# The first chunk of a Mamba scan and the end of a graph attention layer, reordered in a four-layer graph network kernel

## Chip, cores and metric

One Trainium2 chip, one of its cores. The metric is the device time of one execution in microseconds (us); a kernel is told by the median of its runs.

## The reference, cut to what matters

Four layers, each followed by a residual and a layer norm. N is 2048 nodes, the width is 128, all float32. The change touches the end of layer 2 (a dense graph attention) and layer 3 (a graph convolution that feeds a Mamba block).

```
def _L2_gnn_ref(h, adj, weight, a_l, a_r, b):
    x = h @ weight
    scores = (x @ a_l)[:, None] + (x @ a_r)[None, :]
    attn = jnp.where(adj != 0, jnp.exp(leaky_relu(scores, 0.2)), 0.0)
    return attn / jnp.maximum(attn.sum(-1, keepdims=True), 1e-12) @ x + b

def _L3_gnn_ref(x, adj, ...):            # D_INNER 256, D_STATE 16, DT_RANK 8, D_CONV 4
    h = layernorm(relu(adj @ x @ gcn_w + gcn_b)) * ln_g + ln_b
    xc, z = split(h @ w_in)
    u = silu(causal_conv(xc, conv_w) + conv_b)
    dbc = u @ w_xp                       # 8 columns for dt, 16 for B, 16 for C
    dt = softplus(dbc[:, :8] @ w_dt + b_dt)
    hst = exp(dt * A) * hst + dt * B * u # over the 2048 rows, 256 channels x 16 states
    y = sum over states(hst * C) + u * D_skip
    return (y * silu(z)) @ w_out

x = layernorm(x + _L2_gnn_ref(...)); x = layernorm(x + _L3_gnn_ref(...))
```

## The kernel before, in words

The order of the work is written out by hand for each engine: TensorE (PE), VectorE (DVE), ScalarE (ACT), GpSimd (POOL) and the DMA queue of SyncE (SP). Each engine runs its own list in order, and semaphores (`then_inc`, `wait_ge`) tie the lists together.

**Layer 2.** For each of 16 tiles of source nodes `jt`, ACT and DVE make a tile `q2[jt % 4]` of attention weights (128 x 2048), and PE multiplies it into the sums of all 16 output tiles `it` (L899, 128 x 129: the 129th column is the row's sum of weights). The sums lie in PSUM banks 0 to 5, three output tiles to a bank. `l2_mm` is counted up for each bank in the pass of the last `jt`. Then `norm(2, ...)` on DVE works by quarters of four tiles: `after_layer2(q)` forms the factors `zi` and adds the scaled sums to `X` (L1236 to L1243), the statistics follow (L1132, L1135), ACT makes the root (L480, L482), and the scaled rows are `x_ready` (ACT, L486, for quarters 0 to 2; DVE, L1120, for quarter 3). The quarter's rows are scaled only behind the next quarter's residual. Quarter 0 waits for two banks, quarter 1 for all six.

**Layer 3.** The rows are cut into four chunks of 512. `a_part(c, ...)` on PE is adj @ x for a chunk (L913: 16 products of 128 x 512), `a_copy`, `gcn`, `relu`, `h_spread` (statistics, DVE L1263, L1266), `inverse_root` (ACT L589, L591), a scaling (`h_rescale` on DVE for chunk 0, `h_scale` on ACT, L624, for the later ones, with offsets from the DVE's `offset`, L1289), `h_fill` (transposes), `ht_copy` (L596), `conv_part` (L939: 4 taps for each of two blocks of 128 channels), `u_out` (L605), `dbc_product`, `dbc_copy`, `dt_product` (L965), and softplus as `dt_abs` (L665), `dt_log` (L671, L673) and `softplus` (DVE, L1301).

The recurrence runs in steps `k`: 16 states in each of 4 chunks, 64 in all (`n` is the step within its chunk). It needs dt and dt*u "doubled": each block of 64 channels stands in both halves of the 128 partitions, since one instruction handles two states. `dt2` and `du2` are those copies. Before the change both are made by DMA (`by_blocks`): four transfers for each block of 128 channels of dt, on ACT's queue in chunk 0 and SP's later, and as many for du = dt*u on SP's queue. A step is: `decay` on ACT (L688, twice), `make_dbu` on POOL (L445), `scan` on DVE (L1318, twice), `weigh` by C (DVE L1329, or POOL L457 for 3 steps in 8), and `add_up` on PE (L1006). For DVE's `weigh` PE spreads the row of C over the partitions (`spread`, L987), from three bfloat16 `piece`s of dbc that are taken off one after another (`take_off`, L959).

PE, ACT and DVE carry the preparation of the next chunk (`next_chunk`) and of the chunk after it (`chunk_after`, `a_part` in the portions `cuts`) between the steps; what goes at which step `n` is a hand-written table. At the start of a chunk `gated` (L1358) reads the finished sums, then `y_done` lets PE start the next chunk's sums with the skip products (L997), and `out_product` (L976), `residual` and an `o_scale` finish the old chunk.

Of the kernel before, what the change touches and what calls it, by code (L numbers as in the profile page):

```python
# [14 lines left out]
P = 128  # L15
N = 2048
NT = N // P
# [34 lines left out]
def gnn_program(nc, t, out):  # L52
    ctx = ExitStack()
    with ctx:  # L54
# [147 lines left out]
        dt2_in, du2_in = [sem("dt2_in%d" % b) for b in range(DI)], [sem("du2_in%d" % b) for b in range(DI)]  # L202
# [58 lines left out]
        w_dt = wt[:, 11:13, :].rearrange("p a m -> p (a m)")  # L261
# [48 lines left out]
        def doubled(done, c, b):  # L310

            return done[b] if c == 0 else done[0], 64 * (c + 1)
        HF_BANKS = (4, 5, 7)

        def act_features(jt):

            return sum(i % 4 < 2 for i in range(jt + 1))

# [3 lines left out]
        def later_loads(sp):  # L322
# [16 lines left out]
            sp.dma_start(w_dt[96:96 + DTR, :], t["L3_gnn_w_dt"]).then_inc(w4_in, 16)  # L339
            sp.dma_start(w_dt[96 + DTR:97 + DTR, :], t["L3_gnn_b_dt"].rearrange("(o f) -> o f", o=1)).then_inc(w4_in, 16)  # L340
# [32 lines left out]
            for c in range(NCH):  # L373
                sp.wait_ge(dbc_ev, c + 1)
                sp.dma_start(b_dram[c], dbc[0:2 * STATES, :]).then_inc(b_out, 16)
                sp.wait_ge(b_out, 16 * (c + 1))
                if c == 0:
                    b_rows(c, 0)
                    for b in range(DI):
                        sp.wait_ge(du_ready, b + 1)  # L380
                        by_blocks(sp, du, du2[0], slice(b, b + 1), du2_in[b])
                    sp.wait_ge(a_mm, 2)
                else:
                    sp.wait_ge(dt_ready, 2 * c + 2)
                    if c >= 2:
                        sp.wait_ge(da_ready, 2 * STATES * (c - 1))
                    by_blocks(sp, dt_, dt2[c % 2], slice(0, DI), dt2_in[0])
                    sp.wait_ge(du_ready, 2 * c + 2)
# [13 lines left out]
        def later_pool(pool):  # L402
# [22 lines left out]
            def make_du(c, b):  # L425

                pool.wait_ge(dt_ready, 2 * c + b + 1)
                pool.wait_ge(u_ready, 2 * c + b + 1)
                if c:
                    pool.wait_ge(*doubled(du2_in, c - 1, b))  # L430
                nc.gpsimd.tensor_tensor(du[:, b, :], dt_[:, b, :], u[:, b, :], ALU.mult).then_inc(du_ready, 1)

            def make_dbu(k):
# [3 lines left out]
                if n < 2:  # L437
                    pool.wait_ge(*doubled(du2_in, c, n))
# [21 lines left out]
            for b in range(DI):  # L460
                make_du(0, b)
            for k in range(3):
                make_dbu(k)
            for k in range(STEPS):
# [7 lines left out]
        def later_act(act):  # L472
# [126 lines left out]
            def u_out(c, b, bank):  # L599

                act.wait_ge(conv_mm, 2 * c + b + 1)
                if c:
                    act.wait_ge(du_ready, 2 * c)
                    act.wait_ge(skip_mm, c)
                nc.scalar.activation(u[:, b, :], PS[:, bank, :], ACT.Silu, bias=conv_b[:, b:b + 1]).then_inc(u_ready, 1)  # L605
# [14 lines left out]

            def shift_and_scale(dst, v, first, count, offsets, done):
# [6 lines left out]
            def h_scale(c, bank):  # L628

                act.wait_ge(h_off, c)  # L630
                shift_and_scale(ag_tiles, PS[:, bank, :].rearrange("p (s f) -> p s f", f=P), 4 * c, 4, dj, h_ready)

            def o_scale(c):

                act.wait_ge(o_off, c + 1)
                shift_and_scale(xo[c], xo[c], 4 * c, 4, bj, x_ready)

            def dbc_copy(c, bank):
# [3 lines left out]
                if c:  # L642
                    act.wait_ge(b_out, 16 * c)
                    act.wait_ge(dt_mm, 2 * c)
# [14 lines left out]
            def dt_abs(c, b, bank):  # L659

                act.wait_ge(dt_mm, 2 * c + b + 1)
                if c:
                    act.wait_ge(du_ready, 2 * c)
                    act.wait_ge(*doubled(dt2_in, c - 1, b))
                nc.scalar.activation(dt_[:, b, :], PS[:, bank, :], ACT.Abs).then_inc(sp_abs, 1)  # L665

            def dt_log(c, b):

                act.wait_ge(sp_abs, 2 * c + b + 1)
                v = dt_[:, b, :]  # L670
                nc.scalar.activation(v, v, ACT.Exp, scale=-1.0).then_inc(sp_exp, 1)  # L671
                act.wait_ge(sp_exp, 2 * c + b + 1)
# [6 lines left out]
            def decay(j):  # L679
# [4 lines left out]
                if n < 2:  # L684
                    act.wait_ge(*doubled(dt2_in, c, n))
# [19 lines left out]
            for b in range(DI):  # L705
                dt_abs(0, b, 6 + b)
            for b in range(DI):
                dt_log(0, b)
                act.wait_ge(dt_ready, b + 1)
# [1292 lines left out]
```

## Time and profile before

| | |
|---|---|
| median of 3 runs | 933.14 us (932.04 to 934.73) |
| time of the profiled execution | 937.67 us |
| its span | 935.8 us |
| busy: PE, DVE, ACT, POOL | 824.3, 690.8, 508.2, 231.0 us |

The span is what the instructions cover; 1.87 us of the profiled execution lie around it. Layer 2's products run from 555.6 us to 616.9 us of the span, layer 3 from 622.1 us to its end. An engine's time between two of its instructions is idle, and the square brackets in a row say how long it was and whose work ended it.

### The profile page before, as it was taken

How to read it: one execution, taken by the hardware profiler on the slowest of the kernel's cores; microseconds unless marked ns; L12 is line 12 of the kernel's file. 1: busy time of each engine (PE TensorE's matmuls, PEld its weight loads, DVE VectorE, ACT ScalarE, POOL GpSimd, SP SyncE). 2: the span in 40 equal slices, each digit the busy share in tenths (PEclk: the TensorE clock that was granted, in tenths of full speed). 3: DMA queues.
4: the chain of work that ended last, by engine and by line, in shares of the span. 5: the costliest groups of instructions: out<-in, count | busy, mean ns of one | idle time of the engine just before them, and what ended most of it. 6: DMA issues, size and time to landing. Idle time of an engine off the chain costs nothing. (4 is left out here: it accounts for less than half of the span.)

```text
span 935.8 us, 11963 instructions
## 1 busy us (share of the span) xinstructions
PE 824.3 (88%) x4196; PEld 523.5 (56%) x4196; DVE 690.8 (74%) x975; ACT 508.2 (54%) x802; POOL 231.0 (25%) x132
## 2 busy tenths in 40 slices
PE   6999988999999999999599989979579889787755
PEld 6755537888888888854354569954223333231211
DVE  2986889999999999427843148851177888989897
ACT  2654537777877777535220147522457666666461
POOL 2000000000000000000020010001368887877992
PEclk9999998999999999999699979989779999897777
DMA  8589975221122021069100000000432715517210
GB/s 278 189 314 330 360 283 224 91 91 44 46 90 90 0 90 45 1 278 423 47 1 0 1 0 1 1 23 1 115 90 58 159 34 139 123 35 164 64 45 11
DMA packets 39360, 102.42 MB, mean 109 GB/s; under 512 B 6122, under 2 KB 11132, under 8 KB 32788
## 3 DMA queue, kind: packets, MB, share of 16 engines
q1 hardware_dynamic: 38116, 100.55, 32.6%
q10 hardware_dynamic: 1200, 1.32, 0.5%
q8 instruction: 23, 0.38, 0.2%
q14 instruction: 21, 0.17, 0.1%
HBM read 75.33 MB, written 18.14 MB: 100 GB/s over the span
## 5 line engine op out<-in xcount | busy, mean ns | idle before, releaser
L1752 PE MATMUL PS<-big 128*128 128x256 f32 x768 | 194.4, 385 | 3.9 <-ACT big L1582 3.8
L221 PE MATMUL PS<-ident,big 128*128 128x128 f32 x1123 | 158.5, 281 | 22.4 <-DMA big<-in_L_gnn_weight 7.3
L221 PEld LDWEIGHTS PS<-ident,big 128*128 128x128 f32 x1123 | 136.9, 146 | 47.2 <-issue 21.3
L445 POOL TENSOR_TENSOR big<-big 128x1024 f32<-128x1024 f32 x64 | 149.9, 2352 | 20.4 <-DVE big L1318 9.2
L1752 PEld LDWEIGHTS PS<-big 128*128 128x128 f32 x768 | 133.9, 191 | 22.1 <-ACT big L1582 7.6
L1582 ACT ACTIVATE big<-PS 128x512 f32<-128x512 f32 x192 | 105.0, 598 | 58.3 <-PE PS L221 57.3
L1318 DVE TENSOR_TENSOR_SCAN big<-PS,stripes,big 128x512 f32<-128x512 f32 x96 | 116.3, 1260 | 3.6 <-POOL big L445 3.1
L404 POOL MEMSET big<- 128x16 f32 x1 | 0.1, 127 | 465.2 <-DVE big L1120 465.2
L1951 DVE SCALAR_TENSOR_TENSOR big<-big,rz 128x2048 f32<-128x2048 f32 x48 | 112.7, 2350 | 0.9
L1929 DVE CUSTOM_DVE_ANT_0 big<-big 128x2048 f32<-128x2048 bf16 x48 | 109.7, 2289 | 0.1
L688 ACT ACTIVATE PS<-big,stripes 128x512 f32<-128x512 f32 x128 | 86.2, 686 | 40.9 <-DVE big L1318 40.4
L1572 ACT ACTIVATE big<-big,ymin 128x2048 f32<-128x2048 f32 x48 | 96.3, 2006 | 15.2 <-DVE ymin L1929 14.9
L1006 PE MATMUL PS<-big,stripes 128*64 128x512 f32 x256 | 79.0, 727 | 19.3 <-DVE big L1329 19.2
L320 ACT ACTIVATE big<-PS 128x512 f32<-128x512 f32 (+3 forms) x51 | 29.9, 592 | 78.4 <-PE PS L780 24.0
L913 PE MATMUL PS<-big 128*128 128x512 f32 x128 | 64.0, 641 | 5.2 <-ACT big L486 5.2
L1329 DVE TENSOR_TENSOR big<-PS,big 128x1024 f32<-128x1024 f32 x41 | 49.5, 1206 | 15.9 <-issue 11.0
L780 PE MATMUL PS<-big 128*128 128x512 f32 x128 | 59.6, 618 | 1.4 <-ACT big L320 1.4
L899 PE MATMUL PS<-big 128*128 128x129 f32 x512 | 59.7, 281 | 1.1 <-DVE big L1224 1.1
L899 PEld LDWEIGHTS PS<-big 128*128 128x128 f32 x512 | 59.3, 197 | 1.4 <-issue 1.4
L1675 PE MATMUL PS<-big 128*128 128x512 f32 x128 | 57.8, 597 | 0.0
L1006 PEld LDWEIGHTS PS<-big,stripes 128*64 128x64 f32 x256 | 16.3, 155 | 67.0 <-issue 34.4
L457 POOL TENSOR_TENSOR big<-big 128x1024 f32<-128x1024 f32 x18 | 42.4, 2355 | 15.4 <-DVE big L1318 15.3
(207 smaller groups left out, 1002.0 us busy)
## 6 DMA issues: line engine op xcount, KB each, us to landing
big<-in_adj SPq DMA_DIRECT2D x16, 2048.0 KB, 9.0
big<-at_dram SPq DMA_DIRECT2D x4, 4096.0 KB, 27.3
at_dram<-big SPq DMA_DIRECT2D x3, 4096.0 KB, 16.6
big<-b_dram SPq DMA_DIRECT2D x32, 256.0 KB, 4.4
big<-big SPq DMA_DIRECT2D x24, 256.0 KB, 4.7
big<-b_dram SPq DMA_DIRECT2D x36, 128.0 KB, 4.0
at_dram<-big SPq DMA_DIRECT2D x1, 3072.0 KB, 18.8
big<-e_dram SPq DMA_DIRECT2D x3, 1024.0 KB, 6.8
```

What stands on the lines that cost most here:

```text
L221: return nc.tensor.transpose(PS[:, bank, col:col + P], src, ident[:])
L445: nc.gpsimd.tensor_tensor(dbu[k % 3], du2[c % 2][:, 2 * (n % 2):2 * (n % 2) + 2, :], bb[group % 2][:, pair_of(k) % 2, :].unsqueeze(1).to_b ...
L688: nc.scalar.activation(PS[:, 5 + j % 3, :], dt2[c % 2][:, q, :], ACT.Exp, scale=na[:, q, pair_of(k):pair_of(k) + 1]).then_inc(da_ready, 1)
L899: m = nc.tensor.matmul(sums(it, slice(0, P + 1)), q2[jt % 4][:, it * P:(it + 1) * P], x2[:, jt, :], start=(jt == 0 and it % 3 == 0), stop= ...
L913: m = nc.tensor.matmul(PS[:, bank, :], X[:, jt, :], AT[:, jt, c * CH:(c + 1) * CH], start=(jt == 0), stop=(jt == NT - 1))
L1006: m = nc.tensor.matmul(PS[h * HALF:(h + 1) * HALF, 2 + n % 2, :], fold, v[:, h, :], start=False, stop=(n >= STATES - 2), skip_group_check= ...
L1318: nc.vector.tensor_tensor_scan(hs[k % 3][:, b, :], PS[:, 5 + j % 3, :], dbu[k % 3][:, b, :], state[:, pair_of(k), 2 * (n % 2) + b:2 * (n % ...
L1572: e = nc.scalar.activation(w[s], w[s], ACT.Exp, bias=ymin[:, s:s + 1], scale=-1.0, accum_out=zsum[:, s:s + 1])
L1582: nc.scalar.activation(qt[v % 4], PS[:, v % 4, :], ACT.Copy).then_inc(qt_ready, 1)
L1752: m = nc.tensor.matmul(PS[:, 4 + k // 3, 0:256], hw[:, jt, h, :], qt[v % 4][:, 256 * c:256 * c + 256], start=(h == 0 and jt == 0), stop=(h ...
L1929: m = nc.vector.tensor_tensor_reduce(out=w[s], in0=bm[2 * pair + j], in1=eb[0][h], scale=1.0, scalar=3.0e38, op0=ALU.add, op1=ALU.min, acc ...
L1951: m = nc.vector.scalar_tensor_tensor(w[s], w[s], rz[:, s:s + 1], aw[pair][:, j, :], ALU.mult, ALU.mult)
```

## The change

It touches four places. (1) Layer 2: PE runs the source tiles 0 to 12 as before, then waits for the weights of the last three together and runs them by output tile, so that the banks finish one after another; DVE's quarter `q` waits for the banks that it reads only. (2) First chunk: the weights of dt are loaded with each block of 64 columns twice, and PE computes dt doubled in four products; softplus works on the four, straight in `dt2[0]`. u is doubled by DMA (SP's queue) as soon as it is there, and POOL multiplies it by dt in place (`first_du`). The DMAs of dt on ACT's queue and of du on SP's are gone in chunk 0. (3) DVE's `h_spread(1, 1)` stands behind `weigh(0)` and no longer ahead of the loop. (4) `offset` is computed on ACT (five small instructions) and no longer on DVE; `h_fill`, `conv_part`, `out_product`, `residual` and the portions of `a_part` move by one step `n`, and from chunk 1 on `h_fill` and `out_product` stand ahead of work that they stood behind.

```diff
             for c in range(NCH):
+                if c == 0:
+                    for b in range(DI):
+                        sp.wait_ge(u_ready, b + 1)
+                        by_blocks(sp, u, du2[0], slice(b, b + 1), du2_in[b])
                 sp.wait_ge(dbc_ev, c + 1)
...
                 if c == 0:
                     b_rows(c, 0)
-                    for b in range(DI):
-                        sp.wait_ge(du_ready, b + 1)
-                        by_blocks(sp, du, du2[0], slice(b, b + 1), du2_in[b])
                     sp.wait_ge(a_mm, 2)
...
+            def first_du(q):
+
+                pool.wait_ge(du2_in[q // 2], 64)
+                pool.wait_ge(dt_ready, dt_count(0, q))
+                nc.gpsimd.tensor_tensor(du2[0][:, q, :], dt2[0][:, q, :], du2[0][:, q, :], ALU.mult).then_inc(du_first, 1)
...
-            for b in range(DI):
-                make_du(0, b)
-            for k in range(3):
+            for k in range(2):
+                for b in range(DI):
+                    first_du(2 * k + b)
                 make_dbu(k)
+            make_dbu(2)
...
+            def offset(offsets, root, count, first, done, nth):
+
+                cols = slice(first, first + 4)
+                nc.scalar.activation(offsets[:, cols], mv[:, cols, 0], ACT.Copy, scale=-1.0).then_inc(done, 1)
+                act.wait_ge(root, count)
+                act.wait_ge(done, 2 * nth - 1)
+                for i in range(first, first + 4):
+                    m = nc.scalar.activation(offsets[:, i:i + 1], offsets[:, i:i + 1], ACT.Copy, scale=rstd[:, i:i + 1])
+                m.then_inc(done, 1)
...
-            for b in range(DI):
-                dt_abs(0, b, 6 + b)
-            for b in range(DI):
-                dt_log(0, b)
-                act.wait_ge(dt_ready, b + 1)
-                by_blocks(act, dt_, dt2[0], slice(b, b + 1), dt2_in[b])
-            for p in range(3):
-                piece(0, p, 4)
-            for j in range(3):
-                decay(j)
+            for q in range(3):
+                dt_abs(0, q, FIRST_DT[q])
+                dt_log(0, q)
+                piece(0, q, 4)
+                if q:
+                    decay(q - 1)
+            dt_abs(0, 3, FIRST_DT[3])
+            dt_log(0, 3)
+            decay(2)
             a_copy(1, 1)
             relu(1, 1)
...
-                if n == 0:
+                if n == (1 if c == 1 else 0):
                     inverse_root(h_var, c + 1, 4 * c, 4, h_log, h_root)
-                elif n == 1:
+                    offset(dj, h_root, c + 1, 4 * c, h_off, c)
+                if n == 1:
                     h_scale(c, 1)
...
+            LAST = 3
+            for jt in range(NT - LAST):
                 pe.wait_ge(q2_ready, jt + 1)
                 pe.wait_ge(l2_xev, jt // 4 + 1)
                 for it in range(NT):
...
+            pe.wait_ge(q2_ready, NT)
+            for it in range(NT):
+                for jt in range(NT - LAST, NT):
+                    m = weighted(jt, it)
+                if it % 3 == 2 or it == NT - 1:
+                    m.then_inc(l2_mm, 1)
...
-            for b in range(DI):
-                dt_product(0, b, 6 + b)
+            for q in range(4):
+                dt_product(0, q, FIRST_DT[q])
             pe.wait_ge(sel_ready, 6)
+            a_part(1, 1, 8, 10)
             take_off(0, 0, 4)
-            a_part(1, 1, 8, 9)
+            a_part(1, 1, 10, 12)
             take_off(0, 1, 4)
-            a_part(1, 1, 9, NT)
+            a_part(1, 1, 12, NT)
...
                 if n == 1:
-                    h_fill(c, 1)
-                elif n == 2:
                     if c >= 2:
                         pe.wait_ge(zg_ready, 3 * (c - 1))
-                    conv_part(c, 0, 0, range(0, 1))
+                    h_fill(c, 0)
+                elif n == 2:
+                    conv_part(c, 0, 0, range(0, 2))
                 elif n == 3:
-                    conv_part(c, 0, 0, range(1, 4))
-                elif n == 4:
+                    conv_part(c, 0, 0, range(2, 4))
                     if c >= 2:
                         pe.wait_ge(o_added, c - 1)
-                    conv_part(c, 1, 1, range(TAPS))
+                    conv_part(c, 1, 1, range(0, 1))
+                elif n == 4:
+                    conv_part(c, 1, 1, range(1, TAPS))
...
-            cuts = {6: (0, 2), 7: (2, 4), 8: (4, 6), 9: (6, 9), 10: (9, 12), 11: (12, 14), 12: (14, 16)}
+            cuts = {6: (0, 2), 7: (2, 4), 8: (4, 6), 9: (6, 8), 10: (8, 10), 11: (10, 13), 12: (13, 16)}
...
                 if spreads(k):
                     spread(k)
+                if n == 1 and 0 < c < NCH - 1:
+                    next_chunk(c + 1, n)
                 for i in sums_at(k):
                     add_up(i)
-                if c and n == 2:
+                if c < NCH - 1 and (n != 1 or c == 0):
+                    next_chunk(c + 1, n)
+                if c and n == 1:
                     pe.wait_ge(yg_ready, c)
...
-                if q < 2:
-                    dve.wait_ge(l2_mm, 2 if q == 0 else 6)
+                banks = ((0, 1), (2,), (3,), (4, 5))[q]
+                dve.wait_ge(l2_mm, banks[-1] + 1)
...
-            for b in range(DI):
-                softplus(0, b, 6 + b)
+            for q in range(4):
+                softplus(0, q, FIRST_DT[q])
             scan(0)
-            h_spread(1, 1)
             for k in range(STEPS):
                 c, n = k // STATES, k % STATES
                 if k + 1 < STEPS:
                     scan(k + 1)
                 if not on_pool(k):
                     weigh(k)
+                if k == 0:
+                    h_spread(1, 1)
...
-                if c and n == 3:
+                if c and n == 2:
                     dve.wait_ge(o_mm, c)
...
-                if c and n == 5:
-                    offset(bj, o_root, c, 4 * (c - 1), o_off)
-                if c < NCH - 1:
-                    if n == 0:
-                        offset(dj, h_root, c + 2, 4 * (c + 1), h_off)
-                    elif n == 8 or n == 9:
-                        softplus(c + 1, n - 8, 0)
+                if c < NCH - 1 and (n == 8 or n == 9):
+                    softplus(c + 1, n - 8, 0)
```

## Rows read from the trace of the kernel before

**Rows 1.** The page, part 2: DVE's busy tenths in 40 slices.

```profile
DVE  2986889999999999427843148851177888989897
```

**Rows 2.** Windows: busy time of each engine, then PEclk, DMA share, GB/s.

```profile
656.00:675.00 19.00, 8.65 (x16) 3.08 (x15) 1.49 (x3) 7.52 (x13) 5.91 (x4) 0.66 0.55 141
...
690.00:739.00 49.00, 46.60 (x124) 15.36 (x120) 40.98 (x38) 31.05 (x59) 42.08 (x20) 0.90 0.42 98
...
880.00:925.00 45.00, 29.12 (x86) 7.81 (x87) 44.03 (x45) 22.48 (x35) 36.28 (x16) 0.73 0.13 32
```

**Rows 3.** Timeline, layer 2 and its end: start, duration, what, [idle before, releaser].

```profile
545.73 0.94 PE L221 MATMUL PS<-ident,big 128*128 128x128 f32 x4 [2.61 <-DVE big L1120]
...
589.83 27.08 PE L899 MATMUL PS<-big 128*128 128x129 f32 x241
...
606.88 2.29 DVE L1224 SCALAR_TENSOR_TENSOR big<-big 128x2048 f32<-128x2048 f32 x1 [1.27 <-ACT big L569]
614.78 0.23 DVE L1236 TENSOR_TENSOR zi<-PS,ci 128x3 f32<-128x3 f32 x2 [5.60 <-PE PS L899]
...
620.42 1.65 ACT L486 ACTIVATE big<-big,bj,rstd 128x128 f32<-128x128 f32 x4 [1.73 <-DVE bj L1114]
...
622.12 17.71 PE L913 MATMUL PS<-big 128*128 128x512 f32 x34 [5.21 <-ACT big L486]
...
622.82 1.65 ACT L486 ACTIVATE big<-big,bj,rstd 128x128 f32<-128x128 f32 x4 [0.33 <-DVE bj L1114]
...
639.00 0.60 ACT L320 ACTIVATE big<-PS 128x512 f32<-128x512 f32 x1 [11.71 <-PE PS L913]
```

**Rows 4.** Windows of one microsecond at low PEclk or a change of it (third last number).

```profile
546.00:547.00 1.00, 0.67 (x4) 0.26 (x2) 0.00 (x0) 0.30 (x1) 0.00 (x0) 0.50 0.03 9
...
621.00:622.00 1.00, 0.00 (x0) 0.00 (x0) 0.96 (x8) 1.00 (x4) 0.00 (x0) 0.53 0.00 0
...
627.00:628.00 1.00, 1.00 (x2) 0.34 (x1) 0.67 (x3) 0.26 (x2) 0.00 (x0) 0.56 0.00 0
```

**Rows 5.** Timeline of all engines, the first chunk's dt and first steps.

```profile
659.49 0.60 ACT L665 ACTIVATE big<-PS 128x512 f32<-128x512 f32 x1 [1.31 <-PE PS L965]
...
662.88 2.47 ACTq L307 DMA_DIRECT2D big<-big  x4
...
665.39 0.63 ACT L671 ACTIVATE big<-big 128x512 f32<-128x512 f32 x1 [3.27 <-issue]
...
669.63 2.34 POOL L445 TENSOR_TENSOR big<-big 128x1024 f32<-128x1024 f32 x1 [0.88 <-DMA big<-big]
...
670.66 0.63 PE L959 MATMUL PS<-big,neg 96*96 96x512 bf16 x1 [10.35 <-ACT big L320]
...
674.90 2.34 DVE L1318 TENSOR_TENSOR_SCAN big<-PS,big 128x512 f32<-128x512 f32 x2 [7.49 <-ACT PS L688]
...
684.39 0.89 DVE L1263 BATCH_NORM_STATS2 stats<-PS 128x6 f32<-128x128 f32 x4 [7.15 <-ACT PS L583]
...
690.40 1.50 ACT L624 ACTIVATE big<-PS,dj,rstd 128x128 f32<-128x128 f32 x4 [1.63 <-DVE dj L1289]
...
694.18 2.07 PE L939 MATMUL PS<-es,ns 128*128 128x512 f32 x2 [0.68 <-ACT es L596]
```

**Rows 6.** Timeline by engine: a DVE stall, and the start of chunk 1.

```profile
707.50 1.23 DVE L1329 TENSOR_TENSOR big<-PS,big 128x1024 f32<-128x1024 f32 x1 [3.71 <-issue]
...
750.48 3.54 PE L997 MATMUL PS<-ns,wt 128*128 128x512 f32 x4 [3.69 <-DVEq L1360]
...
750.88 1.50 ACT L624 ACTIVATE big<-PS,dj,rstd 128x128 f32<-128x128 f32 x4 [1.59 <-DVE dj L1289]
...
756.02 1.23 DVE L1329 TENSOR_TENSOR big<-PS,big 128x1024 f32<-128x1024 f32 x1 [0.45 <-DVE big L1318]
...
769.14 1.23 DVE L1329 TENSOR_TENSOR big<-PS,big 128x1024 f32<-128x1024 f32 x1 [1.80 <-issue]
```

**Rows 7.** Groups of instructions by line, 612 us to the end.

```profile
L1289 DVE SCALAR_TENSOR_TENSOR bj<-mv,rstd 128x4 f32<-128x4 f32 x3 | 5.4, 1806 | 0.0
```

## The prediction on record

> **What bounds the kernel now.** I read the page first. DVE is the busiest engine of the last third, and ahead of it, in the three slices from 608 to 679 us, its row falls to 5, 1 and 1 tenths [rows 1]. The chain that ended last covers only the kernel's last steps, so I went by stages and timelines instead. The windows show three regimes: from 656 to 675 no engine is full (PE is busy 8.65 of 19 us, DVE 1.49, ACT 7.52), from 690 to 739 PE is (46.60 of 49), and the last chunk is DVE's (44.03 of 45) [rows 2]. So a microsecond taken from the serial stretches in front counts in full; one given to chunk 0's steps counts only if PE's list is earlier too. All times below are places in the span of before; "earlier" is against them.
>
> **Layer 2's end.** A float32 product stands as two rows, so 241 rows in 27.08 us are 0.225 us a product and 3.6 us a pass of 16 [rows 3]. The products end at 616.9, so the last three passes (48 products, 10.8 us) began at 606.1. The last weights are DVE's at 606.88 + 2.29 = 609.2. New: PE waits for them, 3.1 us idle with nothing to fill it, and ends at 620.0, 3.1 later. But banks 0 and 1 are full after 18 products: 609.2 + 4.05 = 613.25, against 614.78 now [rows 3].
>
> DVE's first quarter then goes as before: 5.64 us from its start to ACT's scaling, which takes 1.65 (614.78 and 620.42 [rows 3]). Inside it the factors of ten columns shrink to three, four instructions still, so I take 0.16 off. `x_ready` comes at 613.25 + 5.5 + 1.65 = 620.4, just after PE's end. PE starts on it at 620.5, not 622.12: 1.6 earlier. The later quarters came 2.4 us apart (620.42 and 622.82 [rows 3]); two new sets of factors (0.9 each, the 614.78 step up to the sums) make it 3.3. At full clock PE eats four products in 3.5, so it does not wait for them.
>
> The clock: the granted clock falls to half (1.2 GHz) at about 621.1 in PE's 5.2 us of idleness, and is back at 2.4 GHz at about 627.9 [rows 4]. PE worked at half rate from 622.1 to 627.9 and lost 2.9 us: 16.9 us up to `a_copy` at 639.00 where 14.0 (0.87 a product) would do. New: this idleness shrinks to 0.5 us, so that loss goes. The 3.1 us of idleness at 606.1 may bring one of its own. In before the clock was at half behind an idleness of 2.61 us, at 546 [rows 3, 4], and behind the 3.69 us ahead of L997, whose four rows took 3.54 us, twice the 0.44 a row of full rate [rows 6]. Both had lighter work in front than full passes. I take that it falls (nearer to the 2.61 and 3.69 than to nothing; 6 in 10), with half rate for some 3.5 us as in that L997 row: 1.7 us lost. Sum: 1.6 + 2.9 - 1.7 = 2.8 earlier. Bounds: 4.5 if it does not fall; 1.5 if it stays low as long as at 622.
>
> The Trainium skill (TensorE: Matmul & The Clock Gate, "Why this matters for your kernels") warns against idle gaps between bursts of matmuls, which bring the clock down. By that rule the new gap is a fault of this change; the rows at 546 and 750 agree as far as they go, though neither is a gap in full passes.
>
> **First chunk: dt and its doubling.** Up to `dbc_copy` nothing changes. ACT's row is now: two `abs`, `exp`, `ln`, then 2.47 us in which it only issues four DMAs, `exp` again at 665.39, DMAs again; PE idles 10.35 us for the first `piece`, DVE scans at 674.90 [rows 5]. New, for one block of dt: `abs` 0.63, `exp` 0.66, `ln` 0.53 to the next, 1.82 in all (0.60 and 0.63 busy [rows 5], plus a semaphore's 0.03). ACT's list from 659.49: four of these, 7.3; three pieces at 0.5 and two decays at 0.6, 2.7; half a microsecond of waiting for `take_off`, behind two products of `a_part`; softplus on DVE 0.7, and 0.2 for its start. That is 670.9: `scan(0)` 4.0 earlier. The two extra dt products cost PE 0.9 each and ACT never waits for them. u's DMAs: its last block is ready about 4 us before 659.49 (dbc products 1.9, copy 0.6, dt product 0.9 and their gaps), the first 3.4 us sooner, a convolution's length: 655.5 and 652.1. Four issues take 2.47, and what was issued up to 665.35 let POOL begin at 669.63 [rows 5], so at most 4.3 to landing: 658.9 and 662.3. POOL needs them at 662.2 and 668.0. They are hidden; the second would cost what it exceeds 668 by. B's rows follow u's on the queue and may come 1 to 2 us later than now, near 666, still before dt*u of state pair 0.
>
> POOL then: dt*u of the last block behind the last softplus, 1.26 (half of the elements of L445 at 2.34 [rows 5], and a little), `make_dbu(1)` 2.34: 674.5. That is a new wait of 1.3 us in front of `scan(1)`, queued on DVE; behind it are `weigh(0)` and `h_spread(1, 1)`. PE: with its 10.35 us filled, `a_part` of chunk 1 ends near 669.4, not 680.9. ACT reaches `a_copy` at 670.7, `relu` ends at 674.1. DVE: `scan(1)` 674.5 to 676.85, `weigh(0)` 1.1, `h_spread` 1.25: 679.2. So DVE's 7.15 us in front of L1263 [rows 5] are gone. ACT: root 0.6, `offset` five small instructions 0.7 (my bound: 0.5 if they pipeline, 1.5 at 0.3 each as dependent ones), `h_scale` 1.5: 682.05, against 690.40 + 1.50 = 691.9. Transposes and `ht_copy` as now: convolution at 684.35 against 694.18 [rows 5]. **9.8 earlier.** Bounds: 8.5 (offset 1.5) and 10.5, the shift of DVE's own list.
>
> **Chunk 0's steps** are PE's. DVE stood 3.71 us for `spread(5)` [rows 6], behind the eight taps. The taps start 9.8 earlier, their number before `spread(5)` is the same, and PE still idles twice for 2.4 us ahead of them, so the clock will be low there again. So 9.8 is kept, no more; `cuts` only moves two products from one gap to another. If the clock stays up, up to 2.6 more.
>
> **Starts of chunks 1 to 3.** `h_fill` now stands ahead of `add_up(16)`. In before `y_done` let PE go at 750.48; `h_scale` ended at 752.4. With `offset` 0.7 in ACT's list instead of DVE's, `h_scale` no longer waits 1.59 [rows 6] and ends at 751.5. So PE starts at 751.5, 1.1 later, then: transposes 1.1 and skip 3.5 at half clock, sums 1.1, `out_product` 2.0: `spread(18)` at 759.5, not 755.9, and DVE's `weigh(18)` waits 4 us instead of 0.45 [rows 6]. Most is not lost: in before DVE waited later, 1.80 us at 769.14 for `spread(21)` [rows 6], behind the same PE work. PE itself is 1.1 later plus the clock's 1.0, less 0.7 of its own waiting for `ht_copy`: about 1.4 later. DVE drops `offset` of 1.8 us (mean 1806 ns [rows 7]) and `dj`'s 0.3 to 1.4, but PE binds chunk 1: -1.0. In chunk 2 PE has no `a_part`, DVE binds: I estimate waits 1.0 longer in all by the same count, against the saved 1.8: +0.8. Chunk 3: `out_product` ahead of `spread(50)` costs DVE 2.0, `offset` returns 1.8: -0.2. Sum -0.4, bounds -3.5 and +2.
>
> **Sum.** 2.8 + 9.8 - 0.4 = 12.2 us. The profiled execution took 937.67 us (span 935.8 and 1.87 around it), so 925.5 for its like; the median of the runs shown is 4.53 lower, 933.14, and gives **920.9 us**.
>
> **Rivals.** (a) The forecast, clock down in layer 2's gap: 920.9, chance 0.5. (b) The clock stays up there: 1.7 more, 919.2; if it also stays up in chunk 0, 916.6. PE was at full work before the gap, which speaks for it: 0.25. (c) The chunk starts give back: PE, 4 us late at each of the two, is not absorbed because the `spread` queue runs full, 3 us a start plus chunk 3's: 920.9 + 5.5 = 926.4. For it: PE 46.60 of 49 us busy; against: the 1.8 us already waited for `spread(21)`. 0.17. (d) The doubling does nothing: POOL is bound by B's rows, which stand behind u's eight DMAs, and `make_dbu(0)` starts where it does, 669.63 [rows 5]. Then the two blocks of dt*u (2.5) and `make_dbu(1)` end at 676.9, 2.4 later than forecast, and DVE with them: 923.3. 0.04. (e) Slower: `h_fill` ahead of `add_up` holds all of PE until `h_scale`, and DVE behind it. It decides from 7.7 us of unabsorbed delay at each of two starts (12.6 + 2.8, halved), where the rows give 1.1 for PE and 4 for DVE; `h_scale` would have to end near 758, so two ACT tasks ahead of it would have to wait for scans that themselves wait. Then 936. 0.04.
>
> The range takes (b)'s lower end, less a microsecond for the bounds of `offset` and the starts, and (c) just: 915.5 to 926.5; outside lie (e), the worse half of (c) and sums of bounds, 0.2. Within 0.3% (2.8 us, what a measurement of this kernel tells from no change) lies little of any case: faster 0.93, same 0.03, slower 0.04.
>
> **What would show it.** PE idle for some 3 us near 606, then L899 by tiles with DVE's L1236 four times; L913 starting within 1 us of L899's end, at 2.4 GHz. No DMA issues on ACT between `ln` and `ln`; first L1318 4 us closer to the first L665 (11.4 us, now 15.4), first L939 of chunk 1 24.9 us after it, now 34.7. `weigh(18)` waiting about 4 us on PE, `weigh(21)` hardly. Wrong it would be if the first L1318 waited for a DMA, if L913 still began at half clock, or if DVE's idle time in chunks 1 and 2 grew by more than the some 7 us of L1289 that it drops.

## The result and the profile after

Six runs of the changed kernel (after, for short) have a median of 925.0 us (921.7 to 929.1); six of the kernel before on the same chip have 933.2 (931.5 to 938.2). The ratio is 0.9908, 95% interval 0.9882 to 0.9934: 8.6 us faster (the medians differ by 8.2), where 12.2 were forecast. The ratios of this document go by means and its medians are medians, so a difference can be read in two ways; where the two disagree both are given. 925.0 lies inside the forecast range, 1.5 us below its upper end. One execution of e5 below took 1245.7 us at a mean granted clock of 0.64 and is left out of every figure.

The profiled execution of after took 921.7 us, its span 919.9, the fastest of the six, and 15.9 less than the span of before. Of that, 5.9 us lie ahead of the changed code: the last attention weights of layer 2 end at 603.27 and not at 609.17 (606.88 + 2.29, [rows 3]), though nothing was changed before them. So places in the span can't be compared between two executions; stretches can. From the end of the last weights to the end of the span it is 326.63 us before and 316.63 after. These **10.0 us** are what this pair of executions gives the change.

The page, part 2, DVE's busy tenths in 40 slices of after (before: [rows 1]):

```profile
DVE  3986989999999999517752338872278878889897
```

The hole is shallower: its three slices read 7, 2 and 2 where they read 5, 1 and 1. The timeline of layer 2's end and the first chunk, for all engines (start, duration, what, [idle before, releaser]):

```profile
603.32 10.98 PE L933 MATMUL PS<-big 128*128 128x129 f32 x96 [3.05 <-DVE big L1272]
607.72 0.23 DVE L1284 TENSOR_TENSOR zi<-PS,ci 128x3 f32<-128x3 f32 x2 [4.45 <-PE PS L933]
613.11 1.65 ACT L505 ACTIVATE big<-big,bj,rstd 128x128 f32<-128x128 f32 x4 [1.48 <-DVE bj L1162]
614.81 10.57 PE L956 MATMUL PS<-big 128*128 128x512 f32 x24 [0.50 <-ACT big L505]
628.85 0.60 ACT L326 ACTIVATE big<-PS 128x512 f32<-128x512 f32 x1 [7.18 <-PE PS L956]
...
648.18 3.69 PE L1009 MATMUL PS<-big,wt 9*128 9x512 f32 x8
649.33 0.60 ACT L697 ACTIVATE big<-PS 128x512 f32<-128x512 f32 x1 [1.31 <-PE PS L1009]
651.80 2.78 PE L956 MATMUL PS<-big 128*128 128x512 f32 x4
655.05 0.59 ACT L326 ACTIVATE big<-PS 96x512 bf16<-96x512 f32 x1 [1.51 <-PE PS L1002]
661.59 2.33 DVE L1359 TENSOR_TENSOR_SCAN big<-PS,big 128x512 f32<-128x512 f32 x2
665.54 2.34 DVE L1359 TENSOR_TENSOR_SCAN big<-PS,big 128x512 f32<-128x512 f32 x2 [1.62 <-POOL big L463]
...
670.96 0.85 ACT L650 ACTIVATE dj<-dj,rstd 128x1 f32<-128x1 f32 x4
675.39 3.78 PE L982 MATMUL PS<-es,ns 128*128 128x512 f32 x4 [0.44 <-ACT es L615]
```

Read it against [rows 3] and [rows 5]. PE waits 3.05 us for the last weights, the new gap, and runs the last three source tiles by output tile. DVE starts at 607.72, 4.4 us behind that. PE's wait ahead of the adjacency products is 0.50 us where it was 5.21. The first scan comes 12.26 us behind the first `abs` (15.41 before), and the first convolution of chunk 1 comes 26.06 behind it (34.69 before). ACT issues no DMA between the logarithms.

The start of chunk 1, timeline of PE and DVE of after:

```profile
730.43 1.21 DVE L1400 TENSOR_TENSOR big<-PS,big 128x1024 f32<-128x1024 f32 x1
733.13 1.09 PE L221 MATMUL PS<-ident,big 128*128 128x128 f32 x4 [5.06 <-ACT big L656]
734.01 3.62 PE L1043 MATMUL PS<-ns,wt 128*128 128x512 f32 x4
738.86 2.05 PE L1020 MATMUL PS<-wt,big 128*128 128x128 f32 x16
740.75 0.38 PE L1031 MATMUL PS<-big,sel 96*128 96x512 bf16 x1
741.22 1.23 DVE L1370 TENSOR_TENSOR big<-PS,big 128x1024 f32<-128x1024 f32 x1 [4.42 <-issue]
```

`h_fill` (L221) waits 5.06 us for `h_scale`. Behind it stand the skip products, the sums and `out_product` (L1020), and only then `spread(18)` (L1031), 10.3 us behind `gated` (L1400). In before it was 6.4 us:

```profile
749.15 1.22 DVE L1358 TENSOR_TENSOR big<-PS,big 128x1024 f32<-128x1024 f32 x1
...
755.54 0.38 PE L987 MATMUL PS<-big,sel 96*128 96x512 bf16 x1
```

DVE's `weigh(18)` waits 4.42 us for it (before 0.45, [rows 6]).

The stretches in one table, each from one landmark to the next, in the profiled execution of each kernel. The first scan lies inside the fourth stretch.

| stretch | before | after | earlier | forecast |
|---|---|---|---|---|
| last weights to first adjacency product | 12.95 | 11.54 | 1.41 | 1.6 less 1.7 for the clock |
| to `a_copy` | 16.88 | 14.04 | 2.84 | 2.9 |
| to first `abs` of dt | 20.49 | 20.48 | 0.0 | 0 |
| to the first convolution of chunk 1 | 34.69 | 26.06 | 8.63 | 9.8 |
| to `gated` of chunk 1 | 54.97 | 55.04 | -0.07 | 0 |
| chunk 1 (`gated` to `gated`) | 63.08 | 66.15 | -3.07 | -1.0 |
| chunk 2 | 63.48 | 63.36 | 0.12 | 0.8 |
| chunk 3 and the end | 60.09 | 59.96 | 0.13 | -0.2 |

### The profile page after: what moved, and what is told of

It is laid out like the page before. It is cut to its first block and busy times, and to the rows that moved or that the text cites. A ratio compares the mean times of both kernels' runs of the same rounds, so it can differ in the third digit from the quotient of the medians.

```text
span 919.9 us, 12005 instructions
## 1 busy us (share of the span) xinstructions
PE 816.0 (89%) x4200; PEld 518.7 (56%) x4200; DVE 686.1 (75%) x977; ACT 515.6 (56%) x838; POOL 233.0 (25%) x134
## 5 line engine op out<-in xcount | busy, mean ns | idle before, releaser
L221 PE MATMUL PS<-ident,big 128*128 128x128 f32 x1123 | 158.8, 282 | 34.4 <-ACT big L656 13.3
L221 PEld LDWEIGHTS PS<-ident,big 128*128 128x128 f32 x1123 | 137.3, 146 | 58.0 <-issue 30.2
L956 PE MATMUL PS<-big 128*128 128x512 f32 x128 | 61.6, 619 | 0.5 <-ACT big L505 0.5
L815 PE MATMUL PS<-big 128*128 128x512 f32 x128 | 58.9, 611 | 1.4 <-ACT big L326 1.4
L1712 PE MATMUL PS<-big 128*128 128x512 f32 x128 | 57.8, 596 | 0.0
```

The source lines that it names most:

```text
L221: return nc.tensor.transpose(PS[:, bank, col:col + P], src, ident[:])
L956: m = nc.tensor.matmul(PS[:, bank, :], X[:, jt, :], AT[:, jt, c * CH:(c + 1) * CH], start=(jt == 0), stop=(jt == NT - 1))
```

## The experiments

In the cuts of code, `...` marks lines left out. Two theories of the shortfall. **Theory A**: the order at the chunk starts costs more than forecast (rival (c) in part), since PE stands for `h_scale` with everything behind it. **Theory B**: the first chunk gives less, since PE's clock falls in it. The rival to both is that layer 2's part gives nothing. The kernel before measured 932.1 us (11 runs) beside e1 to e4, 933.0 (22) beside e5 to e8 and 933.9 (11) beside e9 to e11.

**e1, no change to layer 2.** The changed kernel, with layer 2's end as before.

```
-            for jt in range(NT - LAST):
+            for jt in range(NT):
...
-                dve.wait_ge(l2_mm, banks[-1] + 1)
+                if q < 2:
+                    dve.wait_ge(l2_mm, 2 if q == 0 else 6)
```

> The changed kernel with layer 2's end as before. My theory: layer 2's part is worth 4.3 us in the one profile (1.4 us of an earlier start of the first adjacency product, 2.9 us of clock that is no longer lost), so from the last attention weights to the chunk's first a_copy should be 29.8 us again and not 25.6, with the granted clock at half when the adjacency product begins, and the time about 929. Rival: the clock's part differs from run to run, and only the 1.4 us are steady: 926.5, with a stretch of 27 us.

926.4 us (925.4 to 929.7), ratio 0.9942 (0.9923 to 0.9961). Without layer 2's part the change is 1.4 us worse by the medians and 3.2 by the ratios, whose intervals overlap. The stretch from the last weights to `a_copy` takes 29.6 us in its profile, as the theory said; the time is the rival's.

**e2, PE's old order at the chunk starts.** The changed kernel with `h_fill` behind the sums, and `out_product`, `residual`, the root of the finished chunk and the taps at their old steps; chunk 1's own preparation stays as changed.

```
-                if n == 1 and 0 < c < NCH - 1:
-                    next_chunk(c + 1, n)
                 for i in sums_at(k):
                     add_up(i)
-                if c < NCH - 1 and (n != 1 or c == 0):
+                if c and n == 2:
+                    pe.wait_ge(yg_ready, c)
+                    if c < NCH - 1:
+                        pe.wait_ge(ht_ev, c + 2)
+                    out_product(c - 1, 1, range(4), o_mm)
+                if c < NCH - 1:
                     next_chunk(c + 1, n)
-                if c and n == 1:
-                    pe.wait_ge(yg_ready, c)
-                    out_product(c - 1, 1, range(4), o_mm)
...
-                if c and n == 2:
+                if c and n == 3:
                     dve.wait_ge(o_mm, c)
```

> The changed kernel with PE's order at the starts of chunks 1 to 3 as before (h_fill behind the sums, out_product and residual one step later, the taps 1, 3, 4; chunk 1's own preparation and everything else unchanged). My theory: the new order costs 3.1 us in chunk 1 (66.15 us from gate to gate against 63.08) and nothing net in chunks 2 and 3, where it eats what the moved offset saves. So chunk 1 about 63, chunk 2 below 63, chunk 3 a microsecond or two shorter, and 5 us in all: 920. Rival: the loss in chunk 1 is not the order's but PE's backlog of two extra adjacency products in the last cuts and the clock: chunk 1 stays at 65 to 66, time 924.

920.05 us (four runs, 919.2 to 920.8), ratio 0.9863 (0.9845 to 0.9882); this interval and the changed kernel's just touch. Chunks 1, 2 and 3 take 63.06, 61.57 and 58.85 us where the changed kernel has 66.15, 63.36 and 59.96. Theory A holds: the new order costs 6.0 us in these stretches, 5.0 in the medians and 4.2 by the ratios. The other profiles repeat it. From chunk 1's `gated` to the end of the span, the six with the new order (after, e1, e3, e4, e7, e10) take 187.8 to 190.0 us, mean 189.3; the four with the old order and `offset` on ACT (e2, e8, e9, e11) 182.3 to 183.5, mean 182.9; before 186.6.

This profile also shows Theory B's cause, in PE's and ACT's timeline:

```profile
605.07 12.63 PE L933 MATMUL PS<-big 128*128 128x129 f32 x96 [3.04 <-DVE big L1278]
...
651.56 4.96 PE L1009 MATMUL PS<-big,wt 9*128 9x512 f32 x8
656.45 3.78 PE L956 MATMUL PS<-big 128*128 128x512 f32 x4
...
660.70 0.59 ACT L326 ACTIVATE big<-PS 96x512 bf16<-96x512 f32 x1 [3.77 <-PE PS L1002]
```

The 96 rows behind the gap take 12.63 us and not 10.98, and the eight rows of the dt products 4.96 and not 3.69, though they are the same instructions. The windows say why, first e2's and then those of after (third last number: granted clock, 1.00 is 2.4 GHz and 0.50 is 1.2 GHz):

```profile
606.00:607.00 1.00, 1.00 (x7) 1.00 (x7) 0.00 (x0) 0.00 (x0) 0.00 (x0) 0.53 0.07 16
...
609.00:610.00 1.00, 1.00 (x9) 1.00 (x8) 0.00 (x0) 0.00 (x0) 0.00 (x0) 0.76 0.00 0
...
653.00:654.00 1.00, 1.00 (x4) 0.51 (x3) 0.00 (x0) 0.94 (x2) 0.00 (x0) 0.93 0.00 0
654.00:655.00 1.00, 1.00 (x2) 0.42 (x2) 0.33 (x1) 0.99 (x2) 0.00 (x0) 0.50 0.36 129
...
660.00:661.00 1.00, 1.00 (x4) 0.65 (x3) 0.00 (x0) 0.30 (x1) 1.00 (x1) 0.66 0.00 0
```

```profile
606.00:607.00 1.00, 1.00 (x12) 1.00 (x10) 0.00 (x0) 0.00 (x0) 0.00 (x0) 1.00 0.00 0
...
652.00:653.00 1.00, 1.00 (x3) 0.52 (x3) 0.00 (x0) 0.94 (x3) 0.88 (x1) 0.93 0.93 217
653.00:654.00 1.00, 1.00 (x2) 0.22 (x2) 0.43 (x1) 0.54 (x1) 0.39 (x1) 0.50 0.36 96
...
656.00:657.00 1.00, 1.00 (x3) 0.19 (x1) 0.00 (x0) 0.97 (x3) 1.00 (x1) 0.87 0.00 0
```

In e2 the clock fell behind the gap of layer 2, in after it did not. In the first chunk it fell in both, while PE was busy without a pause (1.00 of each microsecond): at about 652.9 in after, with half rate until 656.3, and at 653.9 in e2, until 660.7. `take_off(0, 0)` (L1002) stands behind the slow adjacency products, and ACT waits for it.

**e3, statistics early.** `h_spread(1, 1)` behind `scan(0)` and the root at `n` = 0, where the changed kernel has it behind `weigh(0)` and at `n` = 1.

```
             scan(0)
+            h_spread(1, 1)
...
-                if k == 0:
-                    h_spread(1, 1)
...
-                if n == (1 if c == 1 else 0):
+                if n == 0:
                     inverse_root(h_var, c + 1, 4 * c, 4, h_log, h_root)
```

> The changed kernel with h_spread(1, 1) behind scan(0), and the root and offset of chunk 1 one step earlier on ACT. My theory: the statistics fall into DVE's wait for POOL ahead of scan(1), h_scale ends about 2.5 us earlier, and since PE sets the pace of chunk 0's first half (DVE waits 4.27 us for spread(5)), 2.5 us of it come out: 922.5. Rival: scan(1) comes 0.7 us later and everything of DVE with it, the spread waits shrink by as much only: 925.5.

924.75 us (919.8 to 930.8), ratio 0.9913 (0.9881 to 0.9946): inconclusive. The convolution comes 11.95 us behind the first scan and not 13.80; no gain can be seen at the end.

**e4, the last two tiles.** `LAST = 2`: fewer products by output tile. PE then has no wait for the last weights and one of 2.74 us ahead of the adjacency products instead.

```
-            LAST = 3
+            LAST = 2
```

> The changed kernel with the last two source tiles by output tile and not three. My theory: PE has no wait for weights (3.05 us now), banks 0 and 1 are full 0.8 us earlier, PE ends 3.1 us earlier and then waits about 2.7 us for the first scaled rows: 0.8 us faster if the clock stays up (924.2), 1 to 2 us slower if it falls in that wait (926.5). Rival: the three-tile wait costs clock in some runs, so two tiles is 2 us faster and less spread: 923.

924.6 us (922.6 to 925.2), ratio 0.9909 (0.9893 to 0.9925), no different from the changed kernel. The first adjacency product is 1.1 us earlier (10.47), and the stretch up to `a_copy` takes 15.73 us and not 14.04: the windows show half clock from about 615.2 to 618.6, behind that wait. So one gap is traded for another, and in this profile the clock fell behind it.

**e5, layer 2's change alone**, on the kernel before (the lines of e1 the other way round).

> The kernel before with the end of layer 2 by output tiles alone, all else as before. My theory (layer 2's end gives 1 to 3 us of its own, 2.8 forecast; the run without it lost 1.4 against the whole change): 929.5 to 931, first adjacency product of layer 3 about 11.5 us after the end of the last weights where it was 12.95, and from there to a_copy 14.0 us at full clock where it was 16.9, unless the clock falls in the new gap, which shows as 13.2 and 14.0. Rival (the new gap takes back all that the tiles give): within 0.7 us of 932.1.

931.6 us (eleven runs, 925.3 to 934.6), ratio 0.9963 (0.9935 to 0.9991): the interval does not reach 1, so layer 2's part alone gives something. Of the stretch the profile shows 12.95 + 16.88 - 13.19 - 14.04 = 2.6 us earlier, with the clock fallen in the gap; the medians show 1.4, as e1 did, and the ratio 3.5.

**e6, `h_fill` behind the sums**, `out_product` still at `n` = 1 (the first hunk of e2 alone).

> The changed kernel with h_fill back behind the sums at steps 16 and 32, out_product still at n = 1 ahead of spread(18). Theory A (what chunk 1 lost, gated to gated 66.2 us where the old order has 63.1, comes from PE standing for h_scale with the sums behind it): the stretch falls to about 64 and the median to 921 to 922. Rival B (it is the 2 us of out_product that comes one step too early, ahead of spread(18) and spread(19)): the stretch stays within 0.7 us of 66 and the median within 1 us of the changed kernel's 924.8.

923.2 us (920.9 to 930.7), ratio 0.9893 (0.9848 to 0.9938). Chunk 1 takes 63.66 us: 2.5 of its 3.1 us of loss come from `h_fill`'s place, so the stretch speaks for A; the median lies 1.2 over the upper end of what A gave, and the runs spread too wide to decide. Over the three stretches e6 gains only 2.3 of e2's 6.0 us (187.2 where after has 189.5 and e2 183.5); the rest lies, as far as one profile of each can tell, with `out_product`, `residual` and the taps, which no run takes apart. In this execution alone of all with the new first chunk the clock stayed at 2.4 GHz until 672.5:

```profile
653.20 3.69 PE L1009 MATMUL PS<-big,wt 9*128 9x512 f32 x8
656.83 1.98 PE L956 MATMUL PS<-big 128*128 128x512 f32 x4
658.65 0.38 PE L1002 MATMUL PS<-big,neg 96*96 96x512 bf16 x1
...
659.07 0.59 ACT L326 ACTIVATE big<-PS 96x512 bf16<-96x512 f32 x1 [0.50 <-PE PS L1002]
```

ACT waits 0.50 us for `take_off`, the half microsecond of the forecast. The first scan comes 11.26 us behind the first `abs` (forecast 11.4) and the convolution 25.07 (forecast 24.9).

**e7 and e8, dt products mixed with adjacency products**, on the changed kernel and on e2.

```
-            for q in range(4):
+            pe.wait_ge(sel_ready, 6)
+            for q in range(2):
                 dt_product(0, q, FIRST_DT[q])
-            pe.wait_ge(sel_ready, 6)
-            a_part(1, 1, 8, 10)
+            a_part(1, 1, 8, 9)
+            dt_product(0, 2, FIRST_DT[2])
             take_off(0, 0, 4)
-            a_part(1, 1, 10, 12)
+            dt_product(0, 3, FIRST_DT[3])
+            a_part(1, 1, 9, 12)
             take_off(0, 1, 4)
```

> The changed kernel with PE's list between dbc_copy and take_off(0, 1) mixed: dt products 0 and 1, one adjacency product, dt product 2, take_off(0, 0), dt product 3, three adjacency products. Nothing is added or left out. Theory A (the first scan comes 12.3 to 14.5 us after the first abs, since the granted clock sometimes falls during the four 9-row dt products that stand in a row, and take_off(0, 0) then waits behind two slow adjacency products): first scan at 11.3 to 12.3 us, no wait over 0.3 us of ACT for the piece, median 1 to 2 us below the changed kernel's. Rival B (the place of take_off costs nothing that is not given back, POOL's dt*u sets scan(1) anyway): median within 0.7 us of 924.8.

> The kernel of e2 (the changed kernel with the old order of PE at the starts of chunks 1 to 3) with the mixed order of e7. If both causes are right and add up: 918.5 to 919.5, faster than both kernels by 5 us or more. If the clock only falls elsewhere, or POOL sets scan(1) anyway: e2's 920.05 within 0.7.

e7: 925.95 us (923.9 to 931.1), ratio 0.9921 (0.9896 to 0.9946). e8: 920.5 (917.5 to 924.8), ratio 0.9857 (0.9817 to 0.9898). Neither is better than what it was made from. The clock fell all the same, at 658.8 and 656.1, and `take_off(0, 1)` now stood behind three slow products: ACT waited 2.07 and 3.67 us for it. So it falls without four dt products in a row too, and my new order had a fault of its own.

**e9 and e10, the same with both take_offs first**, on e2 and on the changed kernel.

```
             dt_product(0, 3, FIRST_DT[3])
-            a_part(1, 1, 9, 12)
             take_off(0, 1, 4)
-            a_part(1, 1, 12, NT)
+            a_part(1, 1, 9, NT)
```

> e8 with its fault mended: take_off(0, 1) stood behind three adjacency products there, and ACT waited 2 to 3.7 us for it. Now both take_offs stand ahead of the adjacency products: dt products 0 and 1, one adjacency product, dt product 2, take_off(0, 0), dt product 3, take_off(0, 1), then the other seven. Theory (what spreads the first scan from 11.3 to 14.5 us behind the first abs is PE at half clock working off adjacency products ahead of a take_off): ACT waits for no piece whatever the clock does, the first scan comes 10.8 to 11.2 us behind the first abs in the profile, and the median is 1.5 to 2.5 us below e8's 920.5, so 918 to 919. Rival (POOL and PE's own list set the later steps, so that the earlier scan is only waited out): first scan as said, median within 0.7 us of 920.5.

> The changed kernel with the same mended order as e9 and its own order at the chunk starts. First scan 10.8 to 11.2 us behind the first abs, gated to gated of chunk 1 still 65 to 66 us. By the theory the median is 1.5 to 2.5 us below the changed kernel's 925.0, so 922.5 to 923.5; by the rival within 0.7 us of it. Against e9 of the same call it shows once more what the chunk starts cost: 4 to 5 us.

e9: **918.4 us** (916.5 to 921.0), ratio 0.9832 (0.9804 to 0.9859). e10: 925.3 (923.7 to 926.8), ratio 0.99 (0.9874 to 0.9926). e10 is no better than the changed kernel, so there the rival is right; e9 is 2.1 below e8 and 1.6 below e2, but the intervals overlap. e10's timeline shows where an earlier scan goes:

```profile
657.44 8.77 PE L956 MATMUL PS<-big 128*128 128x512 f32 x14
...
662.75 2.33 DVE L1360 TENSOR_TENSOR_SCAN big<-PS,big 128x512 f32<-128x512 f32 x2
666.69 1.22 DVE L1360 TENSOR_TENSOR_SCAN big<-PS,big 128x512 f32<-128x512 f32 x1 [1.62 <-POOL big L463]
670.35 1.22 DVE L1360 TENSOR_TENSOR_SCAN big<-PS,big 128x512 f32<-128x512 f32 x1 [2.44 <-ACT PS L722]
```

The first scan is 10.64 us behind the first `abs` and ACT waits for no piece. But the last seven adjacency products take 8.77 us, 6.1 at full rate (0.87 each), `a_copy` stands in ACT's list ahead of the next decays, and DVE waits 2.44 us for one of them. The convolution comes 26.97 us behind the first `abs`, later than in the changed kernel (26.06). Between e9 and e10 only the chunk starts differ: 6.9 us in the medians.

**e11, the first chunk alone.** The changed kernel with the edits of e1 and of e2 both: the doubling and `offset` on ACT are left.

> The changed kernel with layer 2's end as before and PE's old order at the chunk starts; what is left of the change is the first chunk (doubled dt and u, h_spread behind weigh) and offset on ACT. If the parts add up as the runs so far say (first chunk 7 to 8.6 us, offset on ACT 1.2 to 1.9 us in each of chunks 2 and 3): 921 to 922. Rival (the parts hide each other, the first chunk alone gives less than 7 us): over 923.5.

921.8 us (920.2 to 923.7), ratio 0.9866 (0.984 to 0.9893), as expected. This part, with `offset` on ACT, is 3.2 us better than the whole change in the medians and 3.9 by the ratios; the ends of the intervals overlap (0.9882 to 0.9893).

## Why the forecast was right, and what it missed

The mechanism and the sign were right and the range held; the size was 3.6 us short, mostly in two terms. The upper end of the range came from rival (c), and that is the side on which the miss lies. One of the forecast's own signs of being wrong also came true: in chunks 1 and 2 DVE's idle time grew from 6.0 and 7.0 us to 10.9 and 9.5, 7.4 in all, against the "some 7" that it named (L1289 took 5.0 us in these two chunks).

**Layer 2's end: right.** First product 1.41 earlier (1.6 forecast), no half rate behind it (2.84, forecast 2.9). The clock behind PE's new gap, 6 in 10 to fall: of the nine profiles with this gap it fell in five (e2, e3, e5, e6, e7) and stayed up in four (the changed kernel, e8, e9, e10). Where it fell it cost 13.19 - 11.54 = 1.65 us, for which 1.7 was forecast. So rival (b) was what this one profile of after shows. The Trainium skill (TensorE: Matmul & The Clock Gate, "Why this matters for your kernels") says that idle gaps between bursts bring the clock down: the five profiles agree, the other four, with the same 3.04 or 3.05 us of waiting behind full passes, do not. What the part gives in whole runs is less sharp than in the stretches: three pairs with and without it (after and e1, e5 and before, e2 and e11) differ by 1.4, 1.4 and 1.8 us in the medians and by 3.2, 3.5 and 0.3 by the ratios, so the runs can't tell 1.4 from the 2.6 of the stretch. In e5's profile the clock fell 1.1 us behind the first `abs` (before: 2.5), and the convolution of chunk 1 came 1.0 us later; that this takes back part of the gain was only argued.

**First chunk: mechanism right, size off.** The waits came as told but for one, ACT's for `take_off`: POOL in front of `scan(1)` 1.62 us (forecast 1.3), u's DMAs hidden, no wait for B's rows of over 1.02 us, DVE's 7.15 us in front of `h_spread` gone. Where the clock stayed up, in e6, the gain is 34.69 - 25.07 = 9.62 us against 9.8. The term that failed is the half microsecond "behind two products of `a_part`": I priced those, and the rest of `a_part`, at full rate. ACT's wait for `take_off` was 0.50 us in e6 and 1.51, 2.15, 3.77, 2.94 and 2.19 in after, e1, e2, e4 and e11, and in all six the first scan comes 10.8 us and this wait behind the first `abs`. In the other profiles with the first chunk of the change the clock fell in it, and the gain is 8.63 (after), 7.98 (e1), 6.37 (e2), 7.15 (e4) and 7.94 (e11); with e6 the mean of the six is 7.95, 1.85 below the forecast. Before the change the clock fell there too, at 662, but PE was idle from 660.3 to 670.66 [rows 5], and only the tail of it met work. The change fills this idleness with products that then run at half rate. `offset` on ACT took 1.17 us (from 670.68 to `h_scale` at 671.85), 0.47 more than the 0.7 that I took and inside the bounds.

**Chunk 0's steps kept it**: 55.04 us against 54.97.

**Chunk starts: the step that failed**, by 2.4 us: -0.4 forecast, -3.07 + 0.12 + 0.13 = -2.8 measured. It is the sum of two large terms. `offset` off DVE was put at 3.6 us, and with the old order (e2) chunks 2 and 3 are 1.91 and 1.24 us shorter than before, 3.15 in all. The order was put at 1.0, 1.0 and 2.0 us for the three chunks, 4.0 in all, and costs 3.1, 1.8 and 1.1, 6.0 in all; rival (c) would have 5.5 more than the forecast, so it holds in part.

The term that failed is chunk 1's. Its first steps came nearly as forecast: PE starts 2.70 us behind `gated` and not 1.33 (1.1 later forecast), `spread(18)` comes 3.9 later (3.6), DVE waits 4.42 us for it (4). What I had wrong is how much of it is made good. The third `weigh` of the chunk starts 22.03 us behind `gated` (752.46 - 730.43) and not 19.99 (769.14 - 749.15), 2.0 later where 1.4 was counted for PE, and the chunk ends 3.07 later. DVE's own work fell by 1.88 us, and its idle time rose by 4.9 (6.0 of 63 to 10.9 of 66). For the clock I took 1.0. Busy times and granted clock of chunk 1, first of before, then of after, then of e2:

```profile
749.00:812.00 63.00, 55.17 (x170) 19.76 (x170) 57.00 (x65) 42.18 (x83) 52.93 (x24) 0.97 0.42 98
```

```profile
730.00:796.00 66.00, 57.34 (x170) 20.66 (x170) 55.12 (x63) 43.38 (x93) 52.71 (x24) 0.92 0.40 93
```

```profile
735.00:798.00 63.00, 56.27 (x170) 20.01 (x170) 55.22 (x63) 43.63 (x94) 52.92 (x24) 0.95 0.42 98
```

The same 170 rows of PE take 57.34 us and not 55.17, with 8.5 us of half clock while PE is busy against 3.4. But the clock isn't the main part: e2 has 5.8 us of it and its chunk 1 takes 63.06, and e3 and e7, with the new order and only 5.3 and 5.5, take 64.88 and 64.94. So 1.8 us of the 3.1 are there at the clock of e2, and about 1.2 go with the second fall of the clock in after (762 to 765.5). Even these aren't saved where it does not fall: chunk 2 of e3 and e7 takes 65.1 us where after has 63.4. The three stretches together vary by 1 to 2 us from profile to profile of one order, and differ by 6.4 between the means of the two orders.

In sum: 12.2, less 1.85 for the first chunk and 2.4 for the chunk starts, less 0.2 for layer 2 with its clock down (2.6), is 7.8 us, against 8.6 by the ratio.

## What to carry to other kernels

Work that is moved into an idle stretch of PE is to be priced at the clock that stretch has, not at full rate. An instruction that waits for a late input costs everything queued behind it: put it behind the work that is ready (`h_fill` alone, e6: 2.5 us in one chunk; the whole order, e2: 6). And a bundle of edits is worth taking apart: the first chunk with `offset` on ACT, 921.8, beat the whole; with layer 2's part and the old order at the chunk starts it was 920.05 (e2), and with the dt products moved too 918.4 (e9).

## What the runs showed of the hardware that was not expected

- The granted clock fell to 1.2 GHz while PE was busy: in after at 652.9, with one wait of 0.87 us in PE's list from 637.5 on and none behind 645.45; by the windows half rate lasted 3.4 us there and 6.8 in e2. At 644 to 646 PE was busy 0.58 and 0.55 of a microsecond, from 646 on 1.00 of each. In one (e6) of seven profiles of otherwise the same first chunk (after, e1, e2, e3, e4, e6, e11) it stayed at 2.4 GHz until 672.5, when PE stood idle. Mixing the 9-row products with full ones did not keep it up. What brings it down is open.
- The same wait of 3.04 or 3.05 us behind the same full-rate products was followed by a lower clock in five of nine profiles. That is 1.65 us between executions in this place alone; one profile and the median can differ by more than the part of a change that is looked at.
- Five dependent small ACT operations (128x4, then four of 128x1) take 1.17 us. On DVE the same formula took 0.16 us in layer 2 (L1162), where POOL was idle, and 0.33 to 1.84 us in before's recurrence (L1289). Each of its six executions in before began while a POOL instruction ran and ended 0.02 us behind that one's end, as here:

```profile
769.75 2.35 POOL L445 TENSOR_TENSOR big<-big 128x1024 f32<-128x1024 f32 x1
770.28 1.84 DVE L1289 SCALAR_TENSOR_TENSOR bj<-mv,rstd 128x4 f32<-128x4 f32 x1
```

So by these rows the instruction lasts as long as the rest of POOL's; why is not shown. In chunks 2 and 3 it took 4.6 us in all, and with `offset` on ACT 3.15 of them came back (e2).
